# Bulk loads moved behind the first two pairs' transfers, and the late weights' sums moved to a later tick, in a fused two-layer decoder kernel

## The reference

```
x = ln(x + attn0(x))         # 16 heads of 64, softmax, out projection wo
x = ln(x + xattn0(x, ctx))   # one head of 128, with biases
x = ln(x + moe0(x))          # one expert's output times the best gate probability
x = ln(x + attn1(x))         # 16 heads of 8, causal
x = ln(x + xattn1(x, ctx))   # retention: rotated q and k, decay mask, no softmax
x = ln(x + ffn1(x))          # ternary weights, activations rounded to 8 bits, silu(gate) * up
```

## Time and profile before

| | us |
|---|---|
| median of 3 runs | 331.54 |
| lowest and highest | 330.96, 332.5 |
| time of the profiled execution | 331.54 |
| span of the profiled execution | 329.7 |
| TensorE busy (matmul) | 253.7 |
| VectorE busy | 209.2 |
| ScalarE busy | 147.6 |
| GpSimd busy | 72.1 |

### The profile page before, as it was taken

One profiled execution on the slowest core, in us unless ns is written; L12 is line 12 of the kernel. 1 busy time (PEld: TensorE's weight loads), 2 busy tenths in 40 slices (PEclk: granted clock), 3 DMA queues, 4 the chain that ended last, 5 costly groups with the idle time before them and its releaser, 6 DMA issues.

```text
span 329.7 us, 6843 instructions
## 1 busy us (share of the span) xinstructions
PE 253.7 (77%) x2658; PEld 191.9 (58%) x2658; DVE 209.2 (63%) x534; ACT 147.6 (45%) x275; POOL 72.1 (22%) x107
## 2 busy tenths in 40 slices
PE   3578679989998999798967999999887767652430
PEld 3546667978787988686844666666564434240110
DVE  2855996499657995765544666567475756354662
ACT  5962663376339545425322444453344543202651
POOL 5793000000011001443017473252020002021002
PEclk9967999999999999999978999999999896555555
DMA  7994631543142503444000800013000000000011
GB/s 233 393 258 141 139 67 66 137 104 82 67 129 64 129 34 118 103 115 51 2 1 2 155 2 2 2 40 66 3 0 2 1 2 0 0 0 1 0 32 32
DMA packets 27823, 22.86 MB, mean 69 GB/s; under 512 B 19152, under 2 KB 24400, under 8 KB 27088
## 3 DMA queue, kind: packets, MB, share of 16 engines
q1 hardware_dynamic: 27792, 22.43, 25.9%
HBM read 12.20 MB, written 6.03 MB: 55 GB/s over the span
## 4 chain that ended last, share of the span: by engine, by line
PE 47%; DVE 26%; ACT 13%; issue 8%; POOL 3%; DMA 1%; SPq 1%; ACTq 0%; DVEq 0%; POOLq 0%
DVE arena L1096 6%; ACT arena L899 4%; PE PS L516 4%; PE PS L619 3%; PE PS L696 3%; ACT xt L922 3%; PE PS L592 3%; PE PS L718 2%; PE PS L560 2%; PE PS L611 2%; PE PS L702 2%; PE PS L701 2%; PE PS L561 2%; POOL rstd L443 2%; DVE stats L1155 2%
## 5 line engine op out<-in xcount | busy, mean ns | idle before, releaser
L441 POOL TENSOR_SCALAR shift<-mv 128x3 f32<-128x3 f32 (+2 forms) x15 | 3.6, 241 | 233.3 <-DVE mv L1158 233.3
L1096 DVE TENSOR_TENSOR arena<-PS,arena 64x512 f16<-64x512 f32 x64 | 44.1, 690 | 9.2 <-ACT arena L899 8.0
L899 ACT ACTIVATE arena<-PS 64x512 f16<-64x512 f32 x64 | 37.8, 591 | 25.4 <-PE PS L547 24.9
L978 ACT ACTIVATE PT<-PS 128x512 f32<-128x512 f32 x32 | 19.1, 596 | 35.1 <-PE PS L702 34.9
L922 ACT ACTIVATE xt<-res,shift,rstd 128x128 f32<-128x128 f32 x42 | 17.7, 483 | 32.6 <-POOL shift L444 32.5
L1231 DVE TENSOR_REDUCE rowmax<-PS 128x4 f32<-128x512 f32 x32 | 21.9, 686 | 13.1 <-PE PS L704 12.6
L545 PE MATMUL PS<-xh,w0l 128*128 128x256 f32 x64 | 21.0, 329 | 11.8 <-DVE arena L1096 6.2
L912 ACT ACTIVATE PT<-PS 128x512 f32<-128x512 f32 x32 | 19.1, 598 | 15.8 <-PE PS L576 14.5
L1101 DVE TENSOR_REDUCE rowmax<-PS 128x4 f32<-128x512 f32 x32 | 21.7, 682 | 6.5 <-PE PS L561 6.4
L592 PE MATMUL PS<-V,PT 128*64 128x68 f32 x512 | 22.2, 229 | 1.9 <-DVE On L1125 1.9
L574 PE MATMUL PS<-arena 128*128 128x128 f16 x128 | 23.3, 221 | 0.1
(11 more groups left out here) (209 smaller groups left out, 657.0 us busy)
## 6 DMA issues: line engine op xcount, KB each, us to landing
arena<-arena SPq DMA_DIRECT2D x8, 512.0 KB, 4.9
v_piece<-VN SPq DMA_DIRECT2D x8, 512.0 KB, 2.9
V<-v_piece SPq DMA_DIRECT2D x64, 64.0 KB, 2.5
arena<-k_piece SPq DMA_DIRECT2D x4, 192.0 KB, 4.3
arena<-q_piece SPq DMA_DIRECT2D x4, 192.0 KB, 6.4
q_piece<-VN SPq DMA_DIRECT2D x6, 96.0 KB, 1.7
w<-wk SPq DMA_DIRECT2D x2, 256.0 KB, 3.4
w<-wq SPq DMA_DIRECT2D x2, 256.0 KB, 4.5
```

Of the source, the lines that this page charges most:

```text
L899: m = fn(dst[:, a], src[a * 64:(a + 1) * 64], ACT.Copy)
L1096: m = tt(lower[:, a], src[a * 64:(a + 1) * 64], upper[:, a], ALU.subtract)
```

## The change

Two things are moved and nothing is added or taken out. `wo` and `x_tok` are issued behind pair 0's own transfers, the 24 other loads behind pair 1's, which is ahead of pair 2's. The three sums move from tick 0 to tick 11, their matmul from tick 1 to 12, the scales from tick 2 to 13.

```diff
-            sp.dma_start(wo[:], wo0).then_inc(s("ld_wo"), 16)
-            sp.dma_start(xt[:], x_tok).then_inc(s("ld_wo"), 16)
-            sp.dma_start(cT[:], ctx_T).then_inc(s("ld_ctx"), 16)
...
+            def load_first():
+
+                sp.dma_start(wo[:], wo0).then_inc(s("ld_wo"), 16)
+                sp.dma_start(xt[:], x_tok).then_inc(s("ld_wo"), 16)
+
+            def load_rest():
+
+                sp.dma_start(cT[:], ctx_T).then_inc(s("ld_ctx"), 16)
...
+                sp.dma_start(wgu_s[:], wgu).then_inc(s("ld_late"), 16)
+                sp.dma_start(wdn_s[:], wdn).then_inc(s("ld_late"), 16)
...
             for p in range(NPAIR):
                 b = p % 2
...
+                if p == 0:
+                    load_first()
+                if p == 1:
+                    load_rest()
...
-                if t == 1:
+                if t == 12:
                     pe.wait_ge(s("w_abs"), 1)
                     pe.wait_ge(s("masks"), 1)
                     mm(bank(6)[:, 0:3], ones[:], wabs[:, 0:3], start=True, stop=True)\
...
-                if t == 0:
+                if t == 11:
                     dve.wait_ge(s("ld_late"), 32)
...
-                if t == 2:
+                if t == 13:
                     dve.wait_ge(s("pe_wsum"), 1)
```

More of the change, by code:

```diff
@@ new lines, in load_rest @@
+            def load_rest():
+                sp.dma_start(cT[:], ctx_T).then_inc(s("ld_ctx"), 16)
+                for dst, src in ((wx0[:, 0, :], xwq0), (wx0[:, 1, :], xwk0), (wx0[:, 2, :], xwv0),
+                                 (bx0[:, 0:1], xbq0), (bx0[:, 1:2], xbk0),
+                                 (wx1[:, 0, :], xwq1), (wx1[:, 1, :], xwq1s), (wx1[:, 2, :], xwk1),
+                                 (wx1[:, 3, :], xwk1s), (wx1[:, 4, :], xwv1),
+                                 (rot_s[:], rot)):
+                    sp.dma_start(dst, src).then_inc(s("ld_ctx"), 16)
+                sp.dma_start(wgu_s[:], wgu).then_inc(s("ld_late"), 16)
+                sp.dma_start(wdn_s[:], wdn).then_inc(s("ld_late"), 16)
+                for dst, src in ((bvx0[:], xbv0.partition_broadcast(P)), (wge_s[:], wge),
+                                 (bge_s[:], bge.partition_broadcast(P)),
+                                 (w1[:, 0:2, :], wqk1), (w1[:, 2, :], wv1), (b1[:], bqk1),
+                                 (bv1_s[:], bv1.partition_broadcast(P)), (wp1_s[:], wp1),
+                                 (bp1_s[:], bp1.partition_broadcast(P)), (decay_s[:], decay)):
+                    sp.dma_start(dst, src).then_inc(s("ld_mid"), 16)
```

## The result

The change makes the kernel slower: 334.85 us (median of six runs, 333.62 to 338.86) against 331.77 (330.96 to 332.5), a ratio of 1.0087 with a 95% interval of 1.0053 to 1.012. The profiled execution took 333.8 us, one of the shorter ones, with a span of 332.0 against 329.7. The ratio leaves out disturbed executions (the one of 338.86 here), and of the traces of experiments 6 and 7, which are such, little more than landings and waits is taken. From L308 on lines have moved by 3 to 9 (L330 is now L335, L332 L337, L560 L569, L604 L613).

The account below looks back on a forecast made before the run. It saw a start-up with no engine full, TensorE waiting for pair 0's copies behind 24 loads, then VectorE, from tick 3 TensorE, bounding. 331.54 - 3.95 - 1.75 + 4.0 + 1.65 + 0.2 = 331.7 us; range 328.5 to 334.2.

Parts of the forecast that it names:

- Part 1: Start-up: pair 0's copies issue earlier, TensorE's 3.00 us idle time and following half clock vanish; gain 3.95 us, bounds 3.0-4.4.
- Part 2: Ticks 0 to 2: the sums and scale instructions leave VectorE's chain; gain 1.75 us (1.40 plus 0.35), bounds 1.4 and 2.25.
- Where they land: Ticks 11 to 13: sums lie under part 4's stall, else cost 0.65 us; their matmul passes cost 0.2 us in tick 12.
- Part 3: `wo` and `x_tok` behind pair 0 add 1.23 us of issue; pair 1's copies still land in time for `scores_q(8)`, tick 3.
- Part 4: Tick 11: 24 loads ahead of pair 2's copies delay them, so `scores_q(16)` stalls 4.0 us, bounds 2.6 and 5.4.
- The clock: Ticks 12 and 13: half clock on TensorE follows the stall and costs 1.65 us, bounds 0 and 2.7.
- The sum: Whole kernel: 331.54 - 3.95 - 1.75 + 4.0 + 1.65 + 0.2 = 331.7 us.
- D: Tick 11: pair 2's copies serialise behind a full queue, landing at 7.2 us or more, longer half clock; 334.1 us, chance 0.20.

Follow-up runs that it names:

- experiment 6: Changed kernel with the first 14 of the 24 loads ahead of pair 2's copies and the other ten behind them; 333.64 us, ratio 1.0044 to before.
- experiment 7: As experiment 6, but the 14 loads reordered: three largest first, the ten small ones right ahead of pair 2's copies; 328.27 us, ratio 0.9861 to before.
- second trace: The changed kernel run once more, unaltered; 335.76 us, ratio 1.0148 to before.
- experiment 2: Changed kernel with `wo` and `x_tok` behind pair 1's second copy, the 24 loads behind pair 2's, gate/up/down weights first; 323.59 us, ratio 0.9799 to before.
- experiment 3: Changed kernel with `wo` and `x_tok` back at the start of SP's list, the 24 loads left behind pair 1; 334.11 us, ratio 1.0085 to before.

## Why the prediction was wrong

The forecast was 331.7 us and no measurable change; the kernel is 0.9% slower, 334.85, outside the range. Taken by its own steps:

- **Part 1, pair 0's copies: right.** -3.95 forecast, -4.03 measured at tick 0. The second copy landed at 20.9, the first maxima were transposed at 25.9 (forecast 26.0), and the half clock between 25.6 and 28.8 is gone.
- **Part 2, the sums: right.** -1.40 and then 0.35 forecast; -1.38 by tick 3, and -1.63 by tick 4 where they were moved alone.
- **Where they land: right.** They lay under the stall. Without it they and their matmul cost 0.57 us, forecast 0.85.
- **Part 3: wrong, and this is the first step that failed.** It said of pair 1's copies "Nothing waits, with 1.2 us to spare at the worst", the worst being 7.2 us. SP's times were right (copies forecast at 35.9, measured 36.00 and 36.54). But it charged `wo` and `x_tok` only with the 1.23 us of their issue, and put their bytes in the queue at nothing. 7.2 us was no upper bound: it was one landing behind small loads, and here 1 MB stood right ahead. 10.7 us measured, so 2.22 us of waiting where none was forecast.
- **Part 4: the mechanism right, the size too small.** Stall 4.0 forecast, 5.20 and 6.46 in two traces. Of the first one, SP's list came 0.9 us later than forecast (79.00, where 81.38 less the 3.27 of that moment gives 78.11), since one load held it for 1.34 us; the landing was 6.3 instead of 5.8. In the second trace the landing was 7.3. The loads ahead of these copies are the ten small ones, so this is the short end (6.3 to 7.6 us in the four traces that have these ten there). The rule of the Trainium skill (DMA: Bandwidth & Descriptors, Rules for kernel authors), that transfers to disjoint partition halves serialise, leaned to a longer landing. The traces agree with it: pair 1's second copy took 6.3 us when issued 0.84 us behind the first and 5.0 when 1.76 behind (experiments 2 and 3).
- **The clock: right for this wait.** 1.65 forecast. Tick 12 from the first matmul on took 1.67 us more at half clock than with the stall filled, with tick 13 2.0 us; in the second trace 2.8 us, close to the upper bound of 2.7. What the forecast leaned on, that idle times of 2.5 us and more are followed by half clock, held for the long ones only. Between 20 and 100 us of all the traces TensorE's waits of 3.00 to 7.10 us were all followed by it. Of the shorter ones those of 1.46, 1.67, 1.77, 2.15 and 2.32 us were, and those of 1.66 (twice), 1.85, 2.06, 2.22, 2.39 and 2.83 were not, so the length of a wait alone doesn't tell.
- **The sum** is then -4.03 - 1.38 + 2.14 + 7.05 + 0.47 = +4.25 us at tick 31, against +0.15 forecast. Of the 4.1 us between them 2.14 are pair 1's copy, 1.67 are ticks 11 and 12 (7.52 for stall, half clock and sums, against 4.0 + 1.65 + 0.2), and 0.3 are gains of the first ticks that aren't seen by tick 3.
- **Rivals.** D, the slower one, gave 334.1 and comes nearest to the time. In the first trace that is luck: the landing was 6.3 us and the half clock cost 2.0. In the second trace tick 11 went as D says, a landing of 7.3 us and 2.8 us of half clock, but with the wait in tick 3 on top, 2.39 us there, which D has not. The range ended at 334.2 because no case had a second wait in it.

What stays open: what makes the end of the kernel take 165 us in one trace and 168 in another, and what else than the queue's content lengthens a landing. What is shown: the two waits, each removed by its own edit, and the loads right ahead in the queue as the reason of the long landings of 8.7 us and more.

## What to carry to other kernels

When loads are moved out of one transfer's way, list every later transfer with a due time on the same queue, and put the loads behind the one that is urgent, in the stretch where the queue next waits for data; here that turned +0.9% into -2.0%. A transfer's landing time is not a property of the transfer: estimate it from the bytes right ahead of it in the queue, not from the slowest landing seen with other things ahead, and leave a margin, since the same copy behind the same ten small loads took 6.3 to 7.6 us here. The stalls of 5.2 and 6.5 us here cost their own length and then 2.0 and 2.8 us more through half clock; behind waits of 1.5 to 2.8 us half clock came in some traces and not in others, so price it as a chance there.

## What the runs showed of the hardware

Each 512 KB of loads right ahead in SP's queue added 2.2 us to the landing of a 512 KB copy within SBUF, some 240 GB/s, for the first copy of a pair as for the second; 768 KB added 3.5 us to that of pair 2 (9.9 against 6.4, experiments 6 and 7). The issuing of a DMA took SP 0.43 to 0.65 us mostly, but single ones took 1.1 to 2.3 us; what held them was not tried. The same wait of TensorE, 1.66 and 1.67 us in two traces of one program, was followed by half clock in one and not in the other. And the same program's traces differ by 2.2 to 2.5 us at tick 31, by how long these few copies take and by whether and how long half clock follows.
